# Window attention with group norm: x in eight transfers a block, y and output in row order, strided oT, another order of the prologue's transfers

## The chip, the cores and the metric

One core of a Trainium2 chip. The metric is the device time of one execution in microseconds (us); lower is better. The engines are PE (TensorE; PEld its weight loads), DVE (VectorE), ACT (ScalarE), POOL (GpSimd) and SP, which here only issues DMAs. ACT issues DMAs too; ACTq and SPq are their issue queues.

## The reference

```python
# x (8, 56, 88, 192) float32; windows of 7 x 11 tokens, 8 heads of 24
def _gn(v, G=32, eps=1e-05):      # over height, width and the 6 channels of a group
    ...
    return ((g - m) / jnp.sqrt(s + eps)).reshape(v.shape)
def _L0_conv_ref(x, qkv_w, qkv_b, proj_w, proj_b):
    ...
    qkv = xw @ qkv_w + qkv_b
    ...
    attn = jnp.einsum('bhnd,bhmd->bhnm', q, k) / jnp.sqrt(jnp.float32(hd)).astype(q.dtype)
    attn = jax.nn.softmax(attn, axis=-1)
    out = jnp.einsum('bhnm,bhmd->bhnd', attn, v)
    ...
    out = out @ proj_w + proj_b
    ...
return x + _L0_conv_ref(_gn(x), L0_conv_qkv_w, L0_conv_qkv_b, L0_conv_proj_w, L0_conv_proj_b)
```

## The kernel before

The 56 rows of an image are cut in four blocks of 14 rows (two strips of windows). A block has 16 windows of 77 tokens, worked on as eight pairs: a pair of windows, one above the other, is a step `i`, and there are 32 blocks and 256 steps. A block lies in SBUF with 112 partitions: one for each of its 14 rows and 8 window columns, in each of which are 11 tokens (tiles) of 192 channels.

Five engine programs run over the same `i`, each step of each engine working on another stage of the pipeline: x of step i+12 is normalised (POOL, L356, L358), that of i+11 split in two float16 parts (ACT L447, POOL L366, L367), that of i+10 transposed (PE L826) and copied out by ACT (L439). Steps 0, 1 and 2 of a block hold two tiles of x, the others one, as do the projections. For i come the scores (PE L758), their maximum (DVE L632), the transposed scores (L744) and their exponential `probs` (ACT L469); for i-1 probs times v (PE L731, `ps_a`), copied to `num` by ACT (L433). The sums of the exponentials go by DMA through DRAM and come back as inverses spread over 32 partitions each (`den`, `inv`, `inv_all`, SP). For i-8 POOL multiplies (`o`, L345), ACT writes the result's upper float16 part to `oT_hi` (L463) and POOL the lower part to `oT_lo` (L371). The output projection of a block (PE L698 into `ps_b`) starts when the oT of all its eight steps is there; DVE adds x, which is loaded a second time as `y_blk` (L640), and the store goes out from `y_blk`.

Float32 products are made of float16 parts in three to five passes; the weights are scaled and split in the prologue. Group statistics of image 0 are made in the prologue (`x_stat`, DVE L495), those of the others between the steps.

Transfers: ACT issues the x loads (L383) and the output stores (L387) after its `probs`, one of each in every second step; SP issues y (L283), statistics (L290) and the small ones. A block goes in four pieces of 4, 3, 2 and 2 tiles. In memory a row of the image is contiguous, and `x_blk`, `out_blk` and y's source take a block as window column, row, tile and channel, so that partition 14 w + r holds row r of window column w; `x_rows` has it as 8 r + w, in the order of memory. DMA and engine programs are kept in order by semaphores alone; the order of the instructions is that of the code.

```python
STEP_TILES = [(0, 2), (2, 2), (4, 2), (6, 1), (7, 1), (8, 1), (9, 1), (10, 1)]
PIECES = [(0, 4), (4, 3), (7, 2), (9, 2)]
```

## Time and profile before

| | |
|---|---|
| time, median of 3 runs | 1518.98 us (1517.67 to 1539.47) |
| the profiled execution: time, span | 1531.71 us, 1529.9 us |
| busy share: PE, PEld, DVE, ACT, POOL | 89%, 79%, 68%, 67%, 64% |
| granted clock, mean over the span | 0.971 |
| DMA | 170.36 MB, 111 GB/s on the mean |

The profiled execution is 1.8 us longer than its span and 12.7 us longer than the median. The granted clock is TensorE's, as a share of full speed. Idle time of an instruction stands in brackets or after a bar, with "<-" and what ended it; "issue" means that the profile shows nothing that the engine waited for. A window's row has the busy times of PE, PEld, DVE, ACT and POOL in this order, each with its instructions (x). The DMA share is the mean busy share of the core's 16 DMA engines. The prologue (weights, statistics of image 0) takes the first 66 us, the last projections and stores the time from 1490 us on.

### The profile page before, as it was taken

To read this page: it belongs to the slowest core of one execution; us is meant where nothing else is said; L and a number is where in the kernel's file an instruction comes from. 1 tells how busy PE (TensorE), PEld (TensorE's weight loads), DVE (VectorE), ACT (ScalarE), POOL (GpSimd) and SP (SyncE) were. 2 spreads that over 40 slices of the span, in tenths; PEclk is the share of its full clock that TensorE was granted. 3 is DMA by queue.
4 is the path that set the end of the run, shared out by engine and by line. 5 is a ranking of instruction groups with operands and counts; after the bars stand their busy time and mean duration, and the time that the engine had idled before them with its cause. 6 is when DMAs were issued, how large, how long until landed. Compare 5 with 4: busy or idle time off the path is not lost.

```text
span 1529.9 us, 84594 instructions
## 1 busy us (share of the span) xinstructions
PE 1361.8 (89%) x36832; PEld 1210.0 (79%) x36832; DVE 1047.8 (68%) x2227; ACT 1025.4 (67%) x1912; POOL 977.4 (64%) x1532
## 2 busy tenths in 40 slices
PE   0489899999998999999999989998999989999995
PEld 0377788888887888888888878887888878888884
DVE  5677677677766766777667866777667766666662
ACT  1567677766776677776767766776667666767761
POOL 0546766677665766767667776777667576767433
PEclk9999999999999999999999999999999999999997
DMA  7233344444444444444444443544433333433333
GB/s 211 69 95 88 112 114 129 120 118 124 108 128 100 115 129 104 129 107 132 111 114 134 113 108 108 132 123 116 116 99 97 98 95 89 106 95 93 85 84 105
DMA packets 129892, 170.36 MB, mean 111 GB/s; under 512 B 46898, under 2 KB 101490, under 8 KB 128628
## 3 DMA queue, kind: packets, MB, share of 16 engines
q1 hardware_dynamic: 98292, 100.59, 26.8%
q10 hardware_dynamic: 31232, 64.35, 14.0%
q8 instruction: 293, 4.80, 1.3%
q14 instruction: 75, 0.61, 0.1%
HBM read 132.04 MB, written 31.54 MB: 107 GB/s over the span
## 4 chain that ended last, share of the span: by engine, by line
PE 77%; DVE 8%; issue 6%; ACT 3%; POOL 3%; DMA 2%; SPq 1%; ACTq 0%; POOLq 0%; DVEq 0%
PE ps_a L698 13%; PE ps_b L698 13%; PE ps_q L698 11%; PE ps_k L698 11%; PE ps_a L731 10%; PE ps_s L744 8%; PE ps_s L758 5%; PE ps_k L826 4%; PE ps_q L793 3%; DVE neg_max L632 2%; POOL st_root L336 2%; DVE stat L495 2%; ACT probs L469 1%; DMA bias_in<-in_qkv_b 1%; DVE st_dev L510 1%
## 5 line engine op out<-in xcount | busy, mean ns | idle before, releaser
L632 DVE TENSOR_REDUCE neg_max<-ps_s 77x16 bf16<-77x1232 f32 x256 | 369.6, 1444 | 221.9 <-PE ps_s L758 221.1
L371 POOL TENSOR_TENSOR oT_lo<-o,oT_hi 128x308 f16<-128x308 f32 x256 | 193.7, 756 | 321.1 <-ACT oT_hi L463 321.1
L469 ACT ACTIVATE probs<-ps_s,exp_shift,exp_scale 77x1232 f32<-77x1232 f32 x256 | 349.2, 1364 | 9.9 <-PE ps_s L744 9.1
L731 PE MATMUL ps_a<-probs,v_all 77*32 77x77 f32 x8192 | 200.6, 234 | 41.1 <-issue 39.8
L452 ACT ACTIVATE v_all<-ps_a 77x384 f32<-77x384 f32 x256 | 124.9, 488 | 166.5 <-PE ps_a L698 166.4
L698 PE MATMUL ps_a<-wv_hiA,xT 128*128 128x192 f16 x1024 | 218.7, 253 | 2.5 <-issue 1.8
L345 POOL TENSOR_TENSOR o<-num,inv_all 128x308 f32<-128x308 f32 x256 | 216.2, 845 | 4.7 <-DMA inv_all<-den_dram 4.7
L439 ACT ACTIVATE xT<-ps_k 128x448 f16<-128x448 f16 x347 | 209.5, 642 | 8.9 <-PE ps_k L826 8.9
L731 PEld LDWEIGHTS ps_a<-probs,v_all 77*32 77x32 f32 x8192 | 148.7, 110 | 68.8 <-issue 44.4
L698 PE MATMUL ps_b<-wp_hi,oT_hi 128*112 128x192 f16 x694 | 188.1, 271 | 13.0 <-POOL oT_lo L371 6.8
L433 ACT ACTIVATE num<-ps_a 128x308 f32<-128x308 f32 x256 | 109.3, 427 | 133.0 <-PE ps_a L731 118.6
L698 PE MATMUL ps_k<-xT,wqk_hiA 128*128 128x154 f16 x1024 | 193.5, 236 | 0.0
L698 PE MATMUL ps_q<-xT,wqk_hiA 128*128 128x154 f16 x1024 | 186.0, 235 | 0.4 <-issue 0.3
L645 DVE TENSOR_TENSOR q_lo<-ps_q,q_hi 128x308 f16<-128x308 f32 x256 | 123.1, 481 | 89.4 <-PE ps_q L793 86.4
L649 DVE TENSOR_TENSOR k_lo<-ps_k,k_hi 128x308 f16<-128x308 f32 x256 | 123.1, 481 | 87.6 <-ACT k_hi L458 86.7
L458 ACT ACTIVATE k_hi<-ps_k 128x308 f16<-128x308 f32 x256 | 110.1, 430 | 106.5 <-PE ps_k L698 106.5
L698 PE MATMUL ps_b<-wp_lo,oT_hi 128*112 128x192 f16 x694 | 177.3, 255 | 0.2 <-issue 0.2
L698 PE MATMUL ps_b<-wp_hi,oT_lo 128*112 128x192 f16 x694 | 177.5, 256 | 0.0
L358 POOL TENSOR_TENSOR x_norm<-x_norm,rstd_all 112x384 f32<-112x384 f32 (+1 forms) x248 | 162.7, 656 | 19.4
L367 POOL TENSOR_TENSOR x_split<-x_norm,x_split 112x384 f16<-112x384 f32 (+1 forms) x248 | 170.2, 686 | 0.0
L356 POOL TENSOR_TENSOR x_norm<-x_norm,mean_all 112x384 f32<-112x384 f32 (+1 forms) x248 | 163.2, 658 | 4.1 <-issue 4.1
L366 POOL COPY x_split<-x_split 112x128 f16<-112x128 f16 (+1 forms) x248 | 64.1, 258 | 155.2 <-ACT x_split L447 154.8
(148 smaller groups left out, 3854.9 us busy)
## 6 DMA issues: line engine op xcount, KB each, us to landing
inv_all<-den_dram SPq DMA_DIRECT2D x1024, 38.5 KB
x_stat<-in_x SPq DMA_DIRECT2D x24, 504.0 KB, 6.1
x_norm<-in_x ACTq DMA_DIRECT2D x32, 336.0 KB
x_norm<-in_x ACTq DMA_DIRECT2D x64, 168.0 KB
y_blk<-in_x SPq DMA_DIRECT2D x32, 336.0 KB
y_blk<-in_x SPq DMA_DIRECT2D x64, 168.0 KB
out<-y_blk ACTq DMA_DIRECT2D x32, 336.0 KB
out<-y_blk ACTq DMA_DIRECT2D x64, 168.0 KB
```

The source lines that it names most:

```text
L345: nc.gpsimd.tensor_tensor(o32[o % 2][:, :], num[o % NUM_BUFS][:, :], inv_all[o % INV_BUFS][:, :], ALU.mult)\
L356: nc.gpsimd.tensor_tensor(x4, x4, of_group(mean_all, g, tiles), ALU.subtract).then_inc(pool_centred, 1)
L358: nc.gpsimd.tensor_tensor(x4, x4, of_group(rstd_all, g, tiles), ALU.mult).then_inc(pool_norm, 1)
L367: nc.gpsimd.tensor_tensor(xs[:, :, LO:ONE], x_step(x_norm, x_s), xs[:, :, 0:CH], ALU.subtract)\
L371: nc.gpsimd.tensor_tensor(oT_tokens(oT_lo, o), by_column(o32[o % 2]), oT_tokens(oT_hi, o), ALU.subtract).then_inc(pool_oT, 1)
L439: last = nc.scalar.activation(xT_tokens(parity(x_s), t0 + c), xT_psum(x_bank(x_s), c), ACT.Copy)
L452: nc.scalar.activation(v_all[v % V_BUFS][:, :, 0:HD], ps_a[0:TOK, 0:2 * CH].rearrange("p (h d) -> p h d", d=HD), ACT.Copy)\
L469: nc.scalar.activation(probs[i % 2][:, :, :].rearrange("p g (a n) -> p g a n", a=4), scores(), ACT.Exp, bias=exp_shift[0:TOK, :], scale=ex ...
L632: nc.vector.tensor_reduce(neg_max[:, :, :, HD:HD + 1].rearrange("p a g e -> p g (a e)"), scores(), AXIS.X, ALU.max, negate=True).then_inc( ...
L645: tt(heads(q_lo), heads(ps_q), heads(q_hi), ALU.subtract).then_inc(dve_q, 1)
L698: last = mm(dst, lhsT, rhs, start=first and n == 0, stop=n == len(pairs) - 1, skip_group_check=True)
L731: last = mm(o, v_all[s % V_BUFS][:, HEADS * w + NG * j + g, :], probs[s % 2][:, g, at:at + TOK], start=True, stop=True, skip_group_check=True)
```

## The change

The transfers of y and of the output take the block in the order of memory (partition 8 r + w). So that the projection's result comes out in that order, `oT_hi` and `oT_lo` are written with the window column innermost: a step's tokens lie 8 elements of float16 (16 bytes) apart, where they lay in runs of 14. x stays in the old order (partition 14 w + r), but is loaded in eight transfers of 14 partitions and 8448 bytes each, one for each window column, on one semaphore a block; two are issued in each of four consecutive steps, and the first of them waits until POOL has split the whole block before. In the prologue SP sends the qkv bias and the projection's weights ahead of its bias, ACT's second pair of statistics transfers waits for them, and the x of block 1 is issued after the weights are scaled. POOL's normalisation of block 1 waits for DVE's of block 0.

```diff
--- before.py
+++ after.py
@@ -93,7 +93,7 @@
 def window_attention(nc, x, qkv_w, qkv_b, proj_w, proj_b, out):
     x_rows = x.rearrange("b (s r) (w c) d -> (b s) (r w) (c d)", r=ROWS, c=WIN_W)
     x_blk = x.rearrange("b (s r) (w c) d -> (b s) w r (c d)", r=ROWS, c=WIN_W)
-    out_blk = out.rearrange("b (s r) (w c) d -> (b s) w r (c d)", r=ROWS, c=WIN_W)
+    out_rows = out.rearrange("b (s r) (w c) d -> (b s) (r w) (c d)", r=ROWS, c=WIN_W)
     den_dram = nc.dram_tensor("den_dram", (ROW_BUFS, NG, NUM), F32, kind="Internal").ap()
 
     with ExitStack() as ctx:
@@ -170,7 +170,7 @@
         dma_den = [sem(f"dma_den{p}") for p in range(DEN_BUFS)]
         dma_inv = [sem(f"dma_inv{p}") for p in range(DEN_BUFS)]
         dma_inv_all = [sem(f"dma_inv_all{p}") for p in range(INV_BUFS)]
-        dma_x = [[sem(f"dma_x{p}_{k}") for k in range(len(PIECES))] for p in range(2)]
+        dma_x = [sem(f"dma_x{p}") for p in range(2)]
         dma_y = [[sem(f"dma_y{p}_{k}") for k in range(len(PIECES))] for p in range(2)]
         dma_out = [[sem(f"dma_out{p}_{k}") for k in range(len(PIECES))] for p in range(2)]
         dma_stat = [sem(f"dma_stat{p}") for p in range(2)]
@@ -191,9 +191,9 @@
             t0, n = PIECES[k]
             return buf[:, t0:t0 + n, :].rearrange("p c d -> p (c d)")
 
-        def piece_of(rows, c, k):
+        def rows_of(rows, c, k):
             t0, n = PIECES[k]
-            return rows[c, :, :, t0 * CH:(t0 + n) * CH]
+            return rows[c, :, t0 * CH:(t0 + n) * CH]
 
         def stat_landed(g):
             return 16 * (2 * min(g + 1, 2) + 4 * max(g - 1, 0))
@@ -213,8 +213,7 @@
             return bank[:, at:at + 4 * PART].rearrange("p (k v r) -> p k v r", k=4, v=WINS)
 
         def oT_tokens(t, s):
-            at = (s % PAIRS) * 2 * WIN_H
-            return t[parity(s)][:, :, :, at:at + 2 * WIN_H].rearrange("p j c t -> p (j c) t")
+            return t[parity(s)][:, :, :, :].rearrange("p j c (t w) -> p (j c) t w", w=NWC)[:, :, :, s % PAIRS]
 
         def y_bank(r):
             return ps_q if r >= N_PAIRS - PAIRS and r % 2 else ps_b
@@ -238,14 +237,14 @@
             sp.dma_start(wA[:, :], qkv_w[0:CA, :]).then_inc(dma_w, 16)
             sp.dma_start(wB[0:CB, :], qkv_w[CA:CH, :]).then_inc(dma_w, 16)
             sp.dma_start(wB[CB:128, :], qkv_w[CA:CH, :]).then_inc(dma_w, 16)
-            sp.dma_start(bp[:, :], proj_b.rearrange("(a c) -> a c", a=1).broadcast_to([128, CH])).then_inc(dma_w, 16)
             sp.wait_ge(pool_const, 2)
+            b_row = qkv_b.rearrange("(a c) -> a c", a=1)
+            for row in (CB, CB + ROW_G):
+                sp.dma_start(bias_in[row:row + 1, :], b_row).then_inc(dma_rows, 16)
             p_rows = proj_w.rearrange("(j g d) c -> g d j c", g=NG, d=HD)
             for g in range(NG):
                 sp.dma_start(p32[ROW_G * g:ROW_G * g + HD, :, :], p_rows[g, :, :, :]).then_inc(dma_rows, 16)
-            b_row = qkv_b.rearrange("(a c) -> a c", a=1)
-            for row in (CB, CB + ROW_G):
-                sp.dma_start(bias_in[row:row + 1, :], b_row).then_inc(dma_rows, 16)
+            sp.dma_start(bp[:, :], proj_b.rearrange("(a c) -> a c", a=1).broadcast_to([128, CH])).then_inc(dma_w, 16)
             for h in range(2):
                 sp.wait_ge(stat_read, h + 1)
                 for n in range(2):
@@ -280,7 +279,7 @@
                 if r % 2 == 0 and 0 <= c < BLOCKS:
                     k = r // 2
                     reach(sp, dma_out[c % 2][k], 16 * (c // 2))
-                    sp.dma_start(piece(y_blk[c % 2], k), piece_of(x_blk, c, k)).then_inc(dma_y[c % 2][k], 16)
+                    sp.dma_start(piece(y_blk[c % 2], k), rows_of(x_rows, c, k)).then_inc(dma_y[c % 2][k], 16)
                 for h in range(2):
                     g, r = divmod(i + 67 - 16 * h, PAIRS_IMG)
                     if r % 3 == 0 and r <= 9 and 2 <= g < BATCH:
@@ -347,10 +346,12 @@
                 n = i + NORM_LEAD
                 if exists(n) and n >= PAIRS:
                     g = n // PAIRS_IMG
-                    if n % PAIRS_IMG == 0 or n == PAIRS:
+                    if n == PAIRS:
+                        pool.wait_ge(dve_norm0, 3)
+                    if n % PAIRS_IMG == 0:
                         pool.wait_ge(stats_done, g + 1)
-                    if n % 2 == 0:
-                        pool.wait_ge(dma_x[parity(n)][n % PAIRS // 2], 16 * (n // PAIRS // 2 + 1))
+                    if n % PAIRS == 0:
+                        pool.wait_ge(dma_x[parity(n)], NWC * 16 * (n // PAIRS // 2 + 1))
                     tiles = STEP_TILES[n % PAIRS][1]
                     x4 = x_step(x_norm, n).rearrange("p c (g k) -> p c g k", k=GCH)
                     nc.gpsimd.tensor_tensor(x4, x4, of_group(mean_all, g, tiles), ALU.subtract).then_inc(pool_centred, 1)
@@ -376,23 +377,28 @@
 
         @block.scalar
         def _(act):
-            def load_x(c, k):
+            def load_x(c, w):
                 if c == 2:
-                    act.wait_ge(dve_x0, 2 * k + 2)
-                reach(act, pool_x, PAIRS * (c - 3) + 2 * k + 2)
-                nc.scalar.dma_start(piece(x_norm[c % 2], k), piece_of(x_blk, c, k)).then_inc(dma_x[c % 2][k], 16)
+                    act.wait_ge(dve_x0, PAIRS)
+                reach(act, pool_x, PAIRS * (c - 2))
+                nc.scalar.dma_start(x_norm[c % 2][ROWS * w:ROWS * (w + 1), :, :].rearrange("p c d -> p (c d)"), x_blk[c, w, :, :])\
+                    .then_inc(dma_x[c % 2], 16)
+
+            def load_block(c):
+                for w in range(NWC):
+                    load_x(c, w)
 
             def store_y(c, k):
                 act.wait_ge(dve_out, PAIRS * c + 2 * k + 2)
-                nc.scalar.dma_start(piece_of(out_blk, c, k), piece(y_blk[c % 2], k)).then_inc(dma_out[c % 2][k], 16)
+                nc.scalar.dma_start(rows_of(out_rows, c, k), piece(y_blk[c % 2], k)).then_inc(dma_out[c % 2][k], 16)
 
             for h in range(2):
+                if h == 1:
+                    act.wait_ge(dma_rows, 6 * 16)
                 for n in range(2):
                     nc.scalar.dma_start(x_stat[h][:, n * TILES:(n + 1) * TILES, :].rearrange("p c d -> p (c d)"),
                                         x_rows[2 * h + n, :, :]).then_inc(dma_stat[h], 16)
-            for c in range(2):
-                for k in range(len(PIECES)):
-                    load_x(c, k)
+            load_block(0)
 
             def spread(t, rows=slice(0, 128)):
                 return t[rows, :, :, :].rearrange("p a g e -> p (a g) e")[:, :, 0:HD]
@@ -416,6 +422,7 @@
             nc.scalar.activation(wv["Bb"][top, :], wB[top, v], ACT.Copy)
             nc.scalar.activation(spread(wqk["Bb"], low), by_head(bias_in, low), ACT.Copy)
             nc.scalar.activation(wv["Bb"][low, :], bias_in[low, v], ACT.Copy).then_inc(act_w, 1)
+            load_block(1)
             act.wait_ge(stat_var, 1)
             nc.scalar.activation(st_log[:, :], st_var[:, :], ACT.Ln).then_inc(act_log, 1)
             act.wait_ge(act_log, 1)
@@ -469,9 +476,10 @@
                     nc.scalar.activation(probs[i % 2][:, :, :].rearrange("p g (a n) -> p g a n", a=4), scores(),
                                          ACT.Exp, bias=exp_shift[0:TOK, :], scale=exp_scale[0:TOK, :])\
                         .then_inc(act_exp, 1)
-                c, r = divmod(i + 18, PAIRS)
-                if r % 2 == 0 and 2 <= c < BLOCKS:
-                    load_x(c, r // 2)
+                c, r = divmod(i + 19, PAIRS)
+                if r < 4 and 2 <= c < BLOCKS:
+                    load_x(c, 2 * r)
+                    load_x(c, 2 * r + 1)
                 c, r = divmod(i - P_LAG - 2, PAIRS)
                 if r % 2 == 0 and 0 <= c < BLOCKS:
                     store_y(c, r // 2)
@@ -607,14 +615,11 @@
                 copy(xs[:, :, HI2:LO], xs[:, :, CA:CH])
                 tt(xs[:, :, LO:ONE], x_step(x_norm, step), xs[:, :, 0:CH], ALU.subtract).then_inc(dve_x0, 1)
 
-            dve.wait_ge(dma_x[0][0], 16)
+            dve.wait_ge(dma_x[0], NWC * 16)
             normalise(1, 0, 4)
-            dve.wait_ge(dma_x[0][1], 16)
             normalise(2, 4, 3)
             split_rest(0)
             split_rest(1)
-            dve.wait_ge(dma_x[0][2], 16)
-            dve.wait_ge(dma_x[0][3], 16)
             normalise(3, 7, 4)
             for step in range(2, PAIRS):
                 split_rest(step)
```

ACT in a middle block, from one pair of DMA issues on, before: `x_norm` is the loaded x, `in_x` the input.

```order
L383 DMA x_norm<-in_x 112x1x576
L387 DMA out<-y_blk 8x14x384
L433 ACTIVATE num<-ps_a 128x308
L439 ACTIVATE xT<-ps_k 128x4x16x7 x2
L447 ACTIVATE x_split<-x_norm 112x192
L452 ACTIVATE v_all<-ps_a 77x16x24
L458 ACTIVATE k_hi<-ps_k 128x4x77
L463 ACTIVATE oT_hi<-o_1 128x22x14
L469 ACTIVATE probs<-ps_s,exp_shift,exp_scale 77x1232
L433 ACTIVATE num<-ps_a 128x308
```

And after, at the second of the four steps that load:

```order
L384 DMA x_norm<-in_x 14x2112 x2
L393 DMA out<-y_blk 112x384
L440 ACTIVATE num<-ps_a 128x308
L446 ACTIVATE xT<-ps_k 128x4x16x7 x2
L454 ACTIVATE x_split<-x_norm 112x2x192
L459 ACTIVATE v_all<-ps_a 77x16x24
L465 ACTIVATE k_hi<-ps_k 128x4x77
L470 ACTIVATE oT_hi<-o_1 128x308
L476 ACTIVATE probs<-ps_s,exp_shift,exp_scale 77x1232
L384 DMA x_norm<-in_x 14x2112 x2
L440 ACTIVATE num<-ps_a 128x308
```

Each pair of one x load and one store has become two x loads with or without a store, or a store alone; the store's DRAM side of 8 by 14 rows is one of 112, and oT_hi's runs of 14 are one row of 308 elements with a step.

ACT in the prologue, before:

```order
L391 DMA x_stat<-in_x 112x2112 x4
L383 DMA x_norm<-in_x 112x1x768
L383 DMA x_norm<-in_x 112x1x576
L383 DMA x_norm<-in_x 112x1x384 x2
L383 DMA x_norm<-in_x 112x1x768
L383 DMA x_norm<-in_x 112x1x576
L383 DMA x_norm<-in_x 112x1x384 x2
L408 ACT_TABLE_LOAD
L408 ACTIVATE wA<-wA,big_inv 128x192 [waits dve_scales]
```

After, with the waits:

```order
L399 DMA x_stat<-in_x 112x2112 x2
L399 DMA x_stat<-in_x 112x2112 [waits dma_rows]
L399 DMA x_stat<-in_x 112x2112
L384 DMA x_norm<-in_x 14x2112 x8
L414 ACT_TABLE_LOAD
L414 ACTIVATE wA<-wA,big_inv 128x192 [waits dve_scales]
```

Block 1's loads have left this place; they stand behind the last of the weights' ACTIVATEs now, and a wait for the bias and projection weights stands ahead of the second half of the statistics.

## Rows read from the trace of the kernel before

**Rows 1.** The page of the kernel before, parts 1 and 3.

```profile
PE 1361.8 (89%) x36832; PEld 1210.0 (79%) x36832; DVE 1047.8 (68%) x2227; ACT 1025.4 (67%) x1912; POOL 977.4 (64%) x1532
...
q8 instruction: 293, 4.80, 1.3%
```

**Rows 2.** Who PE waited for, 60 to 1485 us: total us, times, longest us.

```profile
PE ps_a L731 <- issue: 39.8, 27, 3.7
...
PE ps_s L744 <- issue: 6.0, 7, 1.6
...
PE ps_k L826 <- issue: 5.2, 5, 2.3
```

**Rows 3.** Windows: us, busy of five engines, clock, DMA share, GB/s; PE's waits.

```profile
1100.00:1400.00 300.00, 283.30 (x7639) 254.34 (x7643) 197.82 (x369) 208.54 (x391) 197.97 (x317) 0.96 0.37 95
1400.00:1485.00 85.00, 83.54 (x2394) 74.78 (x2383) 58.92 (x102) 58.52 (x107) 41.14 (x64) 1.00 0.36 88
...
PE ps_s L758 <- ACT probs L469: 1.4, 7, 0.2
```

**Rows 4.** Timeline of ACT's issues and PE near 630 us; all of L383.

```profile
622.94 0.70 ACTq L383 DMA_DIRECT2D x_norm<-in_x  x1
...
623.68 0.69 ACTq L387 DMA_DIRECT2D out<-y_blk  x1
...
628.63 0.33 PE L731 MATMUL ps_a<-probs,v_all 77*32 77x77 f32 x7
630.72 0.66 PE L731 MATMUL ps_a<-probs,v_all 77*32 77x77 f32 x25 [1.75 <-issue]
...
L383 ACTq DMA_DIRECT2D x_norm<-in_x x128: 683/697/5037, 2.7 to 1398.9; - x128
```

**Rows 5.** Windows: two of the prologue, one at the lower clock.

```profile
742.20:745.40 3.20, 3.20 (x22) 3.11 (x21) 1.80 (x2) 1.15 (x3) 0.74 (x2) 0.50 0.33 83
10.00:17.00 7.00, 0.00 (x0) 0.00 (x0) 0.00 (x0) 0.00 (x0) 0.00 (x0) 1.00 1.03 288
18.50:28.00 9.50, 0.00 (x0) 0.00 (x0) 6.15 (x28) 1.28 (x1) 0.39 (x1) 1.00 0.53 194
```

**Rows 6.** The timeline of ACT and PE at the end of a step.

```profile
1459.25 0.45 ACT L463 ACTIVATE oT_hi<-o 128x308 f16<-128x308 f32 x1
...
1459.60 1.36 ACT L469 ACTIVATE probs<-ps_s,exp_shift,exp_scale 77x1232 f32<-77x1232 f32 x1
...
1461.11 0.32 PE L758 MATMUL ps_s<-k_hi,q_hi 25*128 25x77 f16 x16 [0.20 <-ACT probs L469]
```

**Rows 7.** DMA issues (KB each, us to landing); timeline of the prologue.

```profile
x_stat<-in_x ACTq DMA_DIRECT2D x4, 924.0 KB, 15.6
...
2.71 17.04 ACTq L383 DMA_DIRECT2D x_norm<-in_x  x8
...
21.71 0.35 DVE L559 TENSOR_REDUCE big_parts<-wA 128x1 f32<-128x192 f32 x1 [15.74 <-DMA bias_in<-in_qkv_b]
...
48.01 1.50 DVE L602 TENSOR_TENSOR x_norm<-x_norm,rstd_all 112x768 f32<-112x768 f32 x1
...
55.66 0.96 DVE L602 TENSOR_TENSOR x_norm<-x_norm,rstd_all 112x768 f32<-112x768 f32 x1
```

**Rows 8.** Groups by line and form, and two DVE memsets of the timeline.

```profile
L463 ACT ACTIVATE oT_hi<-o 128x308 f16<-128x308 f32 x256 | 117.6, 459 | 27.9 <-POOL o L345 27.9
L447 ACT ACTIVATE x_split<-x_norm 112x384 f16<-112x384 f32 x96 | 49.6, 518 | 2.4 <-DVE x_norm L602 2.4
...
L439 ACT ACTIVATE xT<-ps_k 128x448 f16<-128x448 f16 x347 | 209.5, 642 | 8.9 <-PE ps_k L826 8.9
...
L371 POOL TENSOR_TENSOR oT_lo<-o,oT_hi 128x308 f16<-128x308 f32 x256 | 193.7, 756 | 321.1 <-ACT oT_hi L463 321.1
...
1.24 0.07 DVE L546 MEMSET v_all<- 77x16 f32 x1
...
5.54 0.07 DVE L553 MEMSET big_parts<- 128x12 f32 x1
```

## The prediction

> **What bounds the kernel now.** I read the groups of PE's instructions first, then who made PE wait, then the ACT stretch between two steps, then the prologue. The work is 256 steps (one pair of windows each) of some 5.5 us between 66 us and 1490 us; PE is busy nearly all of it. In the late stretch from 1400 to 1485 us it is busy 83.54 of 85 us at a granted clock of 1.00; from 1100 to 1400 us only 283.3 of 300 us at 0.96 [rows 3]. So the steady part has two losses: idle time, and time at the lower of the two clock levels.
>
> The idle time has a pattern. Most of PE's waits end with no releaser ("issue"): 39.8, 6.0 and 5.2 us at the three places that hold most, 51.0 us in 39 waits, the longest 3.7 us [rows 2]. No data is missing there. One such wait stands in the middle of a run of 32 equal matmuls: 7 are issued, then nothing for 1.75 us, then the other 25 [rows 4]. What PE lacks is instructions. Queue q8 carried 293 packets with 4.80 MB, 16 KB each [rows 1]: with 36832 matmuls and as many weight loads on PE, that is one packet for every 251 of PE's instructions, so it brings PE's program, one every 5 us. It runs on the same DMA engines as the data. In the example ACT has issued an x load and an output store back to back at 622.94 and 623.68 us [rows 4], some 5 us before the wait. After the last x load, at 1398.9 us [rows 4], there is no wait of this kind up to 1485 us: the one row that the view of waits gives for that stretch is on ACT [rows 3], although stores and y loads go on and the DMA share is unchanged (0.36 against 0.37). So I read these waits as fetches that stand behind a pair of large ACT transfers.
>
> Why those transfers are slow shows in the prologue. From 10 to 17 us only whole-row transfers run (112 partitions on both sides) and the DMA share is 1.03 at 288 GB/s; from 18.5 to 28 us only x pieces run, and the share is 0.53 at 194 GB/s [rows 5]. An x piece uses half of the 16 engines; its DRAM side is written as 8 windows by 14 rows. y pieces and stores have the same shape. On each of these eight engines the queue is twice as long as it need be.
>
> The second thing that bounds a step is ACT's stretch k_hi, oT_hi, probs: they run back to back (oT_hi at 1459.25, probs at 1459.60 us), probs ends at 1460.96 and PE's next scores start at 1461.11 with an idle time of 0.20 us put down to probs [rows 6]. Anything added to oT_hi comes out at the end of the step, in the steps where PE gets there first. PE's L826 transposes are twice as many in three of eight steps, and there PE arrives later.
>
> **The change, part by part.**
>
> *Transfers.* y and output now have 112 rows on both sides, as the transfers of the 1.03 share had, so I take them to run on 16 engines with half the backlog on each. A block's x goes in eight transfers of 14 rows of 8448 bytes instead of four of 112 rows of 1536 to 3072 bytes: two in each of four consecutive steps. Two of them are 28 rows, two on each of 14 engines if the rows are spread evenly, where a piece put 14 rows on each of eight. Bytes per engine and step: before 14 x 3072 = 43 KB at most for each of x and store; after 17 KB and 21 KB. So the longest backlog falls from 86 to 38 KB, and the x load beside a store comes in two steps of eight instead of four. I take two thirds of the 51.0 us away: -34 us. Bounds: 0 (if fetches wait for something else) and -51.
>
> *The clock.* From 742.2 to 745.4 us, with PE busy throughout, the granted clock is 0.50, the level of 1.2 GHz [rows 5]. The mean of 0.96 against 1.00 [rows 3] is 12 us of full-speed work lost in 300 us, some 50 us over the 1300 us like it. Part follows waits on POOL's root of the statistics, which stay, and part is hidden where ACT is last. I take a sixth back, -8 us; bounds 0 and -25.
>
> *ACT's and SP's issue time.* An x piece takes ACT's queue 0.70 us, a store 0.69 [rows 4]. Now there are up to two x issues and a store in a step. Each whole row x issue is smaller; with the price unchanged it is 2.1 us beside a probs of 1.36 us and the wait before num, so at most some 0.5 us late in two of eight steps, 30 us in all if nothing hid it; with half the price nothing. I take 0: PE runs scores and projection before it needs num's bank. The added wait (all of block c-2 split before any of c is loaded) is met one step earlier by POOL; behind it on ACT would stand num and xT. The landing has seven steps, over 30 us, so one wait for eight transfers costs nothing.
>
> *Strided attention output.* ACT writes oT_hi and POOL reads it and writes oT_lo with 16 bytes from element to element instead of runs of 14. The trace has no such ACT or POOL instruction. Nearest rows [rows 8]: a DVE memset of 16 elements that lie 128 bytes apart takes 0.07 us, the same as one of 12 adjacent elements: a strided write at no cost. On ACT, 384 elements into long runs take 518 ns and 308 take 459, 0.78 ns each; by that xT's 448 in 64 runs of 7 should take 568 and take 642, 74 ns or 1.2 ns per run more. Charged to each of 308 single elements it is +0.36 us. So oT_hi costs 0 to +0.36 us; I take 0, by the DVE row, which is the only one with single elements. POOL waits 321.1 us for oT_hi in all, 1.25 us a step [rows 8]; that covers up to so much on its 756 ns. Where POOL is late (27.9 us of ACT's waits for it [rows 8]) a longer L371 adds to it: I take +3 us, bounds 0 and +10.
>
> *Prologue.* DVE's first reduction of the weights starts at 21.71 us, after an idle time ended by the DMA of bias_in [rows 7]. All four statistics transfers of 924 KB and all x pieces were queued beside the weights; ACT's eight x issues alone took 17.04 us [rows 7]. Now two statistics transfers (1.85 MB) and the weights with projection and biases (0.8 MB) come first, 2.65 MB at 288 GB/s [rows 5] = 9.2 us, from 2 us on, with 1.5 us for the last to land: 13 us instead of 21.7, -8.7 us. The second half of the statistics, then 6.4 us of transfer from 12 us on, is there by 20 us and wanted at 23; x block 0 by 25, wanted at 38. ACT issues block 1 after its weight work, where it waits for the variance anyway. POOL now waits for DVE's third normalisation: its first two block 1 steps start some 10 us later in the program, in an idle time of the same length. In exchange DVE's multiply of 768 elements is no longer beside POOL's: 1.50 us against 0.96 [rows 7]; with three more such steps I take -1.5 us. If the cover failed, POOL's two steps (5 us) would be the price. Sum -10, bounds -14 and -4.
>
> *Sum:* -34 - 8 + 0 + 3 - 10 = -49 us against the profiled execution of 1531.7 us. The median of the three timed runs is 12.7 us below it; such waits differ from run to run, and I take -45 against the median of 1519: **1474 us**.
>
> **What the Trainium skill says against it.** [Rows 2 to 4] show 51 us of fetch waits. "Runtime: NRT & Kernel Launch", Instruction fetch mechanics, says of crossing a 16 KiB boundary that it is "mostly hidden"; by that the term of -34 would be 0 and the result 1508 us. The 293 packets of 16 KB agree with its page size, the wait inside a run of matmuls speaks against "mostly hidden" here. "SBUF — State Buffer", on 16-byte cachelines, says that at least two accesses must fall in a line for full bandwidth, and that crossing to a new one at each access costs; oT's new step is exactly 16 bytes. The DVE row speaks against it for writes, with only 16 elements. Its outcome is the rival B.
>
> **The rivals.**
>
> *B, the strided write holds up ACT (ends slower at its upper price).* If each element of oT_hi takes two beats instead of one, the 0.78 ns per element of [rows 8] doubles: +0.24 us. ACT's stretch ends the step in about three quarters of the steps: 256 x 0.75 x 0.24 = +46 us: 1520 us. At the +0.36 us of xT's runs it is +69: 1543; with all steps charged, 1566. It makes the kernel slower than before from +0.23 us on. For it: the back-to-back stretch [rows 6]. Against: the DVE row.
>
> *C, no relief for fetches.* The backlog is not what delays them, or rows of 8448 bytes hold an engine as long as 14 small ones. Only the prologue and the POOL term remain: 1519 - 10 + 3 = 1512 us. For it: in no row is a fetch seen to wait. Against: the quiet stretch after the last x load [rows 3, 4].
>
> *D, POOL becomes the bound.* If L371 grows from 0.76 to 2.0 us or more, it uses up the 1.25 us a step; from there each 0.1 us costs 26 us: at 2.1 us 1500, at 2.3 about 1550.
>
> *E, the change does not do what it says:* y and output still on half the engines because of their SBUF side. Then half of the relief goes: 1495 us.
>
> **Chances.** Forecast 0.50 (with E's near half in its upper end; own range 1455 to 1492), B 0.22, C 0.17, D 0.05, E 0.06. Two per cent is 30 us, about what a measurement of this kernel tells from none: faster means under 1489, slower over 1549. The forecast lies below 1489 nearly always, E and C above it: faster 0.50. B at its lower price, C, E and a little of D are within: 0.38. B with the higher price, or with C (1558), and D: slower 0.12. The range from 1452 to 1545 leaves out about 0.05 below and 0.13 above.
>
> **What would show it.** First DVE reduction at about 13 us and its first multiply of x_norm at 39 instead of 48.01 us: prologue right. PE's "issue" waits at a third of 51 us, and a mean clock near 0.98 from 1100 to 1400: fetch right; unchanged: C. oT_hi's mean of 459 ns: at 460 the forecast, at 700 B. L371 under 1.2 us: no D. x_norm issues under 0.7 us each. Wrong would make it above all an oT_hi over 650 ns, or fetch waits that merely move to other transfers.

## The result and the profile after

The changed kernel takes **1664.7 us** (median of four runs, 1661.7 to 1670.5) against 1518.3 us for the kernel before on the same chip: ratio 1.097, 95% interval 1.093 to 1.102. It is slower by 146 us, far outside the range of the prediction. (Some executions of a kernel run over 1.5 per cent longer than its fastest at a lower clock; the ratios here and below leave them out, the medians don't.)

The page of the changed kernel: its span, the row of busy times, and the chain that ended last.

```profile
span 1659.9 us, 84721 instructions
...
PE 1346.2 (81%) x36832; PEld 1201.2 (72%) x36832; DVE 1045.9 (63%) x2227; ACT 1228.4 (74%) x1912; POOL 1097.6 (66%) x1532
...
PE 38%; ACT 26%; POOL 15%; issue 11%; DVE 4%; ACTq 3%; DMA 2%; SPq 0%; POOLq 0%; DVEq 0%
```

PE, which was busy 89 per cent of the span, is at 81, and it holds only 38 per cent of the chain, where the page of the kernel before has 77. The groups by line show whose work grew; these answer to [rows 8].

```profile
L372 POOL TENSOR_TENSOR oT_lo<-o,oT_hi 128x308 f16<-128x308 f32 x256 | 406.1, 1586 | 462.2 <-ACT oT_hi L470 462.2
...
L470 ACT ACTIVATE oT_hi<-o 128x308 f16<-128x308 f32 x256 | 405.4, 1583 | 33.4 <-POOL o L344 33.4
L476 ACT ACTIVATE probs<-ps_s,exp_shift,exp_scale 77x1232 f32<-77x1232 f32 x256 | 391.0, 1527 | 2.2 <-PE ps_s L749 1.2
...
L344 POOL TENSOR_TENSOR o<-num,inv_all 128x308 f32<-128x308 f32 x256 | 226.1, 883 | 0.0
```

oT_hi went from 459 to 1583 ns, oT_lo from 756 to 1586, with the same 308 elements each. probs, on which nothing was edited, went from a mean of 1.36 us (1364 ns) to 1.53 (1527).

PE's waits from 60 to 1610 us (engine, tile and line, who ended them: us in total, times, longest); they answer to [rows 2].

```profile
PE ps_s L763 <- ACT probs L476: 214.3, 242, 3.8
PE ps_a L736 <- issue: 2.3, 2, 1.7
PE ps_s L749 <- issue: 2.1, 3, 1.4
```

The "issue" waits have nearly gone: 7.2 us over all lines. In their place PE waits for probs in 242 of 256 steps. Here is one step end, the timeline at 700 us (start, duration, engine, idle time before in brackets), to be laid beside [rows 6].

```profile
700.02 0.43 ACT L465 ACTIVATE k_hi<-ps_k 128x308 f16<-128x308 f32 x1 [0.34 <-PE ps_k L703]
700.35 1.58 ACT L470 ACTIVATE oT_hi<-o 128x308 f16<-128x308 f32 x1
701.41 1.55 ACT L476 ACTIVATE probs<-ps_s,exp_shift,exp_scale 77x1232 f32<-77x1232 f32 x1
...
703.10 0.32 PE L763 MATMUL ps_s<-k_hi,q_hi 25*128 25x77 f16 x16 [0.90 <-ACT probs L476]
```

Before, probs started 0.35 us behind the start of oT_hi; now it starts 1.06 us behind. It also lasts 0.16 us (by the means) to 0.19 us (here) longer. Together that is 0.9 us on the stretch that ends the step, and PE's idle time went from 0.20 to 0.90 us. (The record of probs begins before that of oT_hi has ended: by 0.10 us in [rows 6], by 0.52 us here. So not all of the 1.12 us by which oT_hi grew is seen.)

The windows that answer to [rows 3] (window, length, busy PE, PEld, DVE, ACT, POOL, granted clock, DMA share, GB/s):

```profile
1100.00:1400.00 300.00, 253.29 (x7004) 227.33 (x7002) 191.29 (x384) 230.03 (x357) 211.50 (x291) 0.98 0.37 94
1400.00:1485.00 85.00, 72.80 (x2052) 65.59 (x2044) 50.50 (x86) 67.93 (x108) 61.32 (x88) 1.00 0.38 95
```

Even with the clock at 1.00 and no "issue" waits, PE is busy 72.80 of 85 us, where it was 83.54.

The prologue, in the timeline, did what was forecast; it answers to [rows 7].

```profile
13.99 0.35 DVE L567 TENSOR_REDUCE big_parts<-wA 128x1 f32<-128x192 f32 x1 [8.01 <-DMA bp<-in_proj_b]
...
14.64 3.68 ACTq L384 DMA_DIRECT2D x_norm<-in_x  x8
...
40.30 0.96 DVE L610 TENSOR_TENSOR x_norm<-x_norm,rstd_all 112x768 f32<-112x768 f32 x1
```

And the DMA issues by line (durations in ns: least, median, most):

```profile
L384 ACTq DMA_DIRECT2D x_norm<-in_x x256: 320/396/1774, 14.6 to 1481.0; - x128
...
L393 ACTq DMA_DIRECT2D out<-y_blk x128: 322/340/2107, 170.8 to 1657.3; - x128
```

An x issue takes ACT's queue 0.40 us and a store 0.34, where they took 0.70 and 0.69 [rows 4].

### The profile page after: what moved, and what is told of

It reads as the page before. It is cut to its first block, busy times and chain, and to the rows that moved or that the text cites. A ratio compares the mean times of both kernels' runs of the same rounds, so it can differ in the third digit from the quotient of the medians.

```text
span 1659.9 us, 84721 instructions
## 1 busy us (share of the span) xinstructions
PE 1346.2 (81%) x36832; PEld 1201.2 (72%) x36832; DVE 1045.9 (63%) x2227; ACT 1228.4 (74%) x1912; POOL 1097.6 (66%) x1532
## 4 chain that ended last, share of the span: by engine, by line
PE 38%; ACT 26%; POOL 15%; issue 11%; DVE 4%; ACTq 3%; DMA 2%; SPq 0%; POOLq 0%; DVEq 0%
ACT probs L476 15%; PE ps_b L703 11%; ACT oT_hi L470 10%; PE ps_a L703 10%; PE ps_k L703 9%; POOL oT_lo L372 7%; PE ps_s L763 4%; POOL st_root L335 2%; PE ps_q L798 2%; DVE neg_max L637 2%; POOL x_norm L359 2%; POOL x_split L368 2%; POOL x_norm L357 2%; ACTq L384 1%; POOL o L344 1%
## 5 line engine op out<-in xcount | busy, mean ns | idle before, releaser
L372 POOL TENSOR_TENSOR oT_lo<-o,oT_hi 128x308 f16<-128x308 f32 x256 | 406.1, 1586 | 462.2 <-ACT oT_hi L470 462.2
L470 ACT ACTIVATE oT_hi<-o 128x308 f16<-128x308 f32 x256 | 405.4, 1583 | 33.4 <-POOL o L344 33.4
L476 ACT ACTIVATE probs<-ps_s,exp_shift,exp_scale 77x1232 f32<-77x1232 f32 x256 | 391.0, 1527 | 2.2 <-PE ps_s L749 1.2
L763 PE MATMUL ps_s<-k_hi,q_hi 25*128 25x77 f16 x4096 | 84.9, 197 | 219.3 <-ACT probs L476 215.4
L763 PEld LDWEIGHTS ps_s<-k_hi,q_hi 25*128 25x128 f16 x4096 | 56.8, 94 | 259.6 <-issue 252.4
L344 POOL TENSOR_TENSOR o<-num,inv_all 128x308 f32<-128x308 f32 x256 | 226.1, 883 | 0.0
L703 PE MATMUL ps_a<-wv_hiA,xT 128*128 128x192 f16 x1024 | 214.2, 249 | 0.6 <-issue 0.2
L736 PE MATMUL ps_a<-probs,v_all 77*32 77x77 f32 x8192 | 193.9, 234 | 2.4 <-issue 2.3
```

The costliest lines, as they stand in the source:

```text
L344: nc.gpsimd.tensor_tensor(o32[o % 2][:, :], num[o % NUM_BUFS][:, :], inv_all[o % INV_BUFS][:, :], ALU.mult)\
L372: nc.gpsimd.tensor_tensor(oT_tokens(oT_lo, o), by_column(o32[o % 2]), oT_tokens(oT_hi, o), ALU.subtract).then_inc(pool_oT, 1)
L470: nc.scalar.activation(oT_tokens(oT_hi, o), by_column(o32[o % 2]), ACT.Copy).then_inc(act_oT, 1)
L476: nc.scalar.activation(probs[i % 2][:, :, :].rearrange("p g (a n) -> p g a n", a=4), scores(), ACT.Exp, bias=exp_shift[0:TOK, :], scale=ex ...
L703: last = mm(dst, lhsT, rhs, start=first and n == 0, stop=n == len(pairs) - 1, skip_group_check=True)
L736: last = mm(o, v_all[s % V_BUFS][:, HEADS * w + NG * j + g, :], probs[s % 2][:, g, at:at + TOK], start=True, stop=True, skip_group_check=True)
```

## The experiments

Twelve kernels ran. "Theory 1" below is throughout: ACT's f16 write at 16 bytes a step is dear by itself, and costs the step because it stands on ACT's back-to-back stretch.

**The forms by themselves.** No kernel around them: on each engine four instructions in a row of 128 x 308 elements from an f32 tile, for each distance between written elements, with one engine at work at a time. The rest of the computation is left out.

```diff
+ for s in (1, 2, 4, 7, 8, 16):
+     for _ in range(REPEATS):
+         link(act, nc.scalar.activation(every(f16["act"][s], s), src[:, :], ACT.Copy))
+ for s in (1, 2, 4, 8):   # ... the same into f32, then a strided f16 read; DVE and POOL likewise
```

> A kernel that only copies x to the output and, with nothing beside it, runs single operations on 128 x 308 elements one after the other: ACT copies, DVE casts and POOL subtractions that write float16 at a step of 1, 2, 4, 7, 8 and 16 elements and float32 at 1, 2, 4 and 8, and such that read float16 at 1, 4 and 8. It computes nothing of the attention. Theory 1 (a strided write is dear by itself): ACT at step 8 takes about 1.58 us, as oT_hi does in the changed kernel, against 0.46 at step 1; POOL's write at step 8 takes about 1.5 us and its read at most 1.1. Theory 2 (the price comes from ACT and POOL working on lines of the same tile at the same time): ACT at step 8 stays under 0.8 us here. Theory 3 (16-byte lines decide): float16 is cheap up to step 4 and dear from 8, float32 dear from step 4. Theory 4 (any gap decides, single 2-byte writes): float16 is dear from step 2 on and float32 never.

Windows of four instructions each on ACT (window, length, busy time of the four, clock, DMA): f16 written at a step of 1, 2, 4, 8 and 16 elements, and f32 at 8.

```profile
124.40:126.46 2.06, 1.84 (x4) 1.00 0.00 0
126.46:128.79 2.33, 2.19 (x4) 1.00 0.00 0
128.79:132.45 3.66, 3.54 (x4) 1.00 0.00 0
...
138.13:144.51 6.38, 6.25 (x4) 1.00 0.00 0
144.51:150.60 6.09, 5.96 (x4) 1.00 0.00 0
157.68:160.82 3.14, 3.01 (x4) 1.00 0.00 0
```

Divided by four: 460, 547, 885, 1562 and 1490 ns in f16, 753 in f32. The 1562 ns at step 8 (16 bytes) are within 2 per cent of the 1583 of the kernel, without any other engine at work, so theory 2 fell. The same on POOL: f16 at step 1, f16 at step 8, f32 at step 8.

```profile
167.50:171.34 3.84, 3.07 (x4) 1.00 0.00 0
184.41:190.94 6.53, 6.22 (x4) 1.00 0.00 0
207.35:210.76 3.41, 3.10 (x4) 1.00 0.00 0
```

768, 1555 and 775 ns. On DVE a cast of the same shape takes 321 ns at step 1 and 848 at step 8 in f16 (windows of four: 1.28 and 3.39 us), and 443 in f32 at step 8. So the price lies in the write itself, and most of it in the f16 type; neither contention nor the addressing of single elements alone explains it, since POOL writes f32 at 32 bytes for 7 ns more. Theories 3 and 4 both fell too: in f16 ACT's time rises at every distance instead of at one (547 ns at 4 bytes, 885 at 8), and f32 is dearer on ACT (753 ns) and DVE (443) but not on POOL. Why the types differ is open.

**oT in runs, all else as changed.** oT_hi and oT_lo are written in runs of 14 as before while y and output stay in row order, so tokens meet the wrong rows: the output is not the reference's.

```diff
-            return t[parity(s)][:, :, :, :].rearrange("p j c (t w) -> p (j c) t w", w=NWC)[:, :, :, s % PAIRS]
+            at = (s % PAIRS) * 2 * WIN_H
+            return t[parity(s)][:, :, :, at:at + 2 * WIN_H].rearrange("p j c t -> p (j c) t")
```

> The changed kernel with oT_hi and oT_lo written in runs of 14 elements as before, everything else as changed. The projection's rows then meet the y of other tokens, so the output is not the reference's; the amount of work is the same. Theory 1: all of the loss is the strided write and what my prediction gave for the rest holds: 1474 us, between 1455 and 1492, PE's waits without releaser under 20 us. Rival (the new transfers or waits cost too): above 1519 us.

Measured 1495.7 us, ratio to before 0.982 (0.978 to 0.985). The strided oT costs some 170 us (169 between the medians on two chips, 176 by the two ratios), more than the 146 by which the kernel got slower: the rest of the change is worth 1.8 per cent. That is less than expected: the time lies above the range up to 1492, and the "issue" waits above 20 us. PE's "issue" waits from 60 to 1485 us fell from 62.0 us (all lines, the largest in [rows 2]) to 40.5. Its largest rows:

```profile
PE ps_s L750 <- issue: 17.2, 14, 4.4
PE ps_s L764 <- ACT probs L477: 15.3, 16, 2.1
PE ps_a L737 <- issue: 8.5, 7, 2.8
```

**x and prologue as changed, y, output and oT as before.**

```diff
-                nc.scalar.dma_start(rows_of(out_rows, c, k), piece(y_blk[c % 2], k))
+                nc.scalar.dma_start(piece_of(out_blk, c, k), piece(y_blk[c % 2], k))
```

(and the same for y's loads, with oT in runs)

> The changed kernel with y, output and oT as before (8 by 14 rows, runs of 14); only x in eight transfers and the new prologue are left of the change. Prologue alone would give 1519 - 10 = 1509 us. If fetches of instructions wait behind pairs of x load and store, half of those pairs are gone and x is on 14 engines: about 1485 us and some 25 us of PE waits without releaser. If only y and stores mattered: 1509 us and 50 us of such waits.

1524.5 us, ratio 1.002 (0.997 to 1.008), above both 1485 and 1509. First probs came at 65.7 us instead of 75.1, and still nothing was gained; "issue" waits were 62.0 us, as before. So x in eight transfers relieves no fetch, and costs about what the prologue gives.

**Row order and strided oT on the kernel before** (x in four pieces, old prologue).

```diff
-            return t[parity(s)][:, :, :, at:at + 2 * WIN_H].rearrange("p j c t -> p (j c) t")
+            return t[parity(s)][:, :, :, :].rearrange("p j c (t w) -> p (j c) t w", w=NWC)[:, :, :, s % PAIRS]
```

> The kernel before with y and output in row order and the strided oT, x still in four pieces and the old prologue. Theory 1: the strided write is the loss, so it comes out above the changed kernel by the prologue's 10 us: about 1675 us, PE's wait for probs above 200 us. Rival (x in eight transfers or its wait on a whole block carries part of the loss): under 1650 us.

1675.8 us, as theory 1 had it, ratio 1.100 (1.096 to 1.104), with oT_hi at 1584 ns, oT_lo at 1585 and PE waiting 207 us for probs. This part alone makes the whole loss.

**The prologue alone** on the kernel before.

```diff
+            for k in range(len(PIECES)):      # behind ACT's weight work; block 0 stays in front
+                load_x(1, k)
             act.wait_ge(stat_var, 1)
```

(and SP's order, the wait ahead of the second half of the statistics and POOL's wait, as in the change)

> The kernel before with the new prologue alone (SP's order of the weights' transfers, the second half of the statistics behind the projection and biases, x block 1 behind ACT's weight work, POOL's first block 1 step behind DVE's third normalisation); x in four pieces, y and output by window. If the prologue's gain is real and only the eight transfers of x cost time in the run x8_and_prologue (ratio 1.0023 with both), this is 9 to 11 us faster than before: 1508, ratio 0.993, first probs at 65 to 66 us instead of 75.1, and the eight steps of a block add up to 41.0 us as before. If the gain is given back later by something in the steady part whatever x does, it is level: 1518.

1518.3 against 1534.7 us on that chip, ratio 0.989 (0.986 to 0.993): the prologue's gain, 16 us by the ratio (11 to 22), is there and is kept; it is somewhat more than the 9 to 11 expected. First probs at 65.3 us.

**One strided write at a time.** First ACT's alone, with POOL writing oT_lo in runs, so that the lower parts stand at other tokens than the upper ones; then POOL's alone, with ACT writing in runs, so that the upper parts stand at the wrong tokens.

```diff
-                    nc.gpsimd.tensor_tensor(oT_tokens(oT_lo, o), by_column(o32[o % 2]), oT_tokens(oT_hi, o),
+                    nc.gpsimd.tensor_tensor(oT_runs(oT_lo, o), by_column(o32[o % 2]), oT_tokens(oT_hi, o),
```

> The changed kernel, but POOL writes oT_lo in runs of 14 (it still reads oT_hi strided); ACT writes oT_hi strided. The output is not the reference's. Theory 1 (ACT's strided write alone holds the step, since it stands on ACT's back-to-back stretch): oT_hi stays at about 1.58 us, oT_lo falls to 1.0 us, and the time stays within 25 us of the changed kernel, 1640 to 1665. Rival (POOL's own strided write is what the steps wait for, or is needed too): at least half of the 146 us goes, 1590 or less. PE's waits for probs: about 200 us by the first, under 100 by the second.

> The changed kernel, but ACT writes oT_hi in runs of 14 and POOL reads it so; POOL alone writes oT_lo strided. The output is not the reference's. Theory 1 (ACT's write is what costs): oT_hi 460 ns, oT_lo 1.5 to 1.6 us, and the time within 20 us of rows_in_runs' 1496, since POOL had 1.25 us a step to spare. Rival (each strided write alone costs, by a shared path of the two engines or by POOL's pace): 1560 or more, with probs still at 1.5 us.

ACT's alone: 1649.8 us. POOL's alone: 1503.0. The groups of ACT's alone, and its largest wait:

```profile
L474 ACT ACTIVATE oT_hi<-o 128x308 f16<-128x308 f32 x256 | 405.2, 1583 | 30.4 <-POOL o L348 30.4
L480 ACT ACTIVATE probs<-ps_s,exp_shift,exp_scale 77x1232 f32<-77x1232 f32 x256 | 390.7, 1526 | 2.5 <-PE ps_s L753 1.7
L376 POOL TENSOR_TENSOR oT_lo<-o,oT_hi 128x308 f16<-128x308 f32 x256 | 254.2, 993 | 513.8 <-ACT oT_hi L474 513.8
...
PE ps_s L767 <- ACT probs L480: 212.6, 241, 3.5
```

and the groups of POOL's alone:

```profile
L376 POOL TENSOR_TENSOR oT_lo<-o,oT_hi 128x308 f16<-128x308 f32 x256 | 408.2, 1594 | 235.5 <-ACT oT_hi L474 235.3
...
L474 ACT ACTIVATE oT_hi<-o 128x308 f16<-128x308 f32 x256 | 117.6, 459 | 30.7 <-POOL o L348 30.7
```

The first is 15 us below the changed kernel, the second 7 us above the kernel with neither. These are single runs on two chips; set against before on their own chips (medians 1534.7 and 1519.1 us) they are 1.075 and 0.989, beside 0.982 with neither, which gives some 142 us for ACT's write and 12 for POOL's. POOL's instruction grew by 838 ns, but from its start to that of `o` behind it, it is only 1.19 us instead of 0.72, since their records overlap by 0.4 us: some 120 us in all. That found room in idle time: POOL's waits for oT_hi fell from 312.3 us (oT in runs) to 235.3, those for x_split from 134.0 to 93.0. On ACT the start of the next instruction moves by 0.72 us, and there it costs 142 to 154 us. probs is at 1.53 us in the first and not in the second, so it goes with ACT's own strided write ahead of it, not with POOL's beside it. Whether probs works longer, or its record only holds more of the overlap with oT_hi, no run tells apart; PE waits for its end in either case.

**The reordering moved to f32.** The microbenchmark says where the order can be changed for nothing: in POOL's f32 product. o32 becomes a buffer of a whole block in row order, and oT_hi and oT_lo are made tile by tile one step before the projection, both from and to adjacent elements.

```diff
-                    nc.gpsimd.tensor_tensor(o32[o % 2][:, :], num[o % NUM_BUFS][:, :], inv_all[o % INV_BUFS][:, :], ALU.mult)
+                    nc.gpsimd.tensor_tensor(o32_step(o), by_column(num[o % NUM_BUFS]), by_column(inv_all[o % INV_BUFS]), ALU.mult)
...
-                    nc.scalar.activation(oT_tokens(oT_hi, o), by_column(o32[o % 2]), ACT.Copy).then_inc(act_oT, 1)
+                    nc.scalar.activation(oT_tiles(oT_hi, t), o32_tiles(t), ACT.Copy).then_inc(act_oT, 1)
```

Here t = i - 15; o32_step is the strided view of one step, o32_tiles the adjacent view of the one or two tiles that step t of the projection takes.

> The changed kernel with the reordering moved to the f32 product: POOL writes o32 in row order at 32 bytes a step into a buffer of a whole block (in the microbenchmark 775 ns strided against 768), and one step before the projection wants them, ACT and POOL make oT_hi and oT_lo of one or two tiles from and to adjacent elements. Theory 1 (only the f16 writes at 16 bytes were dear): oT_hi's mean is 450 to 480 ns, the first product's stays within 5 per cent of 883 ns, and the time is that of rows_in_runs, 1495 (ratio 0.98). Rival: the strided f32 write is dearer beside the other engines than alone, or PE now waits each step for oT_lo of the step before, 0.2 us a step or more: 1545 or slower, with PE's waits for POOL oT_lo at 50 us.

1498.4 us, ratio 0.978 (0.974 to 0.982), and nothing is left out: the time of the kernel with oT in runs, as theory 1 had it. oT_hi's mean is 451 ns. The rival fell by its own marks (1545 us, 50 us of waits), but it saw something: PE does wait 31.7 us for oT_lo, though most of it in seven waits of 3 us and not in each step.

**The same with x in four pieces and the new prologue.**

```diff
-                    pool.wait_ge(dma_x[parity(n)], NWC * 16 * (n // PAIRS // 2 + 1))
+                    pool.wait_ge(dma_x[parity(n)][n % PAIRS // 2], 16 * (n // PAIRS // 2 + 1))
```

> As g1_staged_rows, but x comes in four pieces as before, with the new prologue. If x in eight transfers costs 0.4 to 0.6 us a block in the steady part (13 to 18 us), this is that much faster than g1_staged_rows: 1478 to 1484, ratio 0.975, and a block's eight steps add up to 40.9 us or less instead of 41.4. If x's eight transfers are what relieves the fetches when y and output take 16 engines, PE's issue waits are back at 60 us and it is at 1495 or above. If the row order of y and output gives the relief, they are 40 us or less.

1489.1 us, ratio 0.970 (0.966 to 0.973): 9 us less than with eight transfers on the same chip, somewhat less than the 13 to 18 expected, and the "issue" waits are 34 us. The row order of y and output gives the relief; x in eight transfers takes some of it back.

**One step of slack.** In that kernel's timeline POOL is late once an image:

```profile
680.21 5.43 POOL L348 TENSOR_TENSOR st_root<-st_var,half_power 112x32 f32<-112x32 f32 x1
...
688.16 1.03 POOL L386 TENSOR_TENSOR oT_lo<-o,oT_hi 128x448 f16<-128x448 f32 x1
...
689.34 0.26 PE L716 MATMUL ps_b<-wp_hi,oT_hi 128*112 128x192 f16 x1 [3.03 <-POOL oT_lo L386]
```

```diff
-P_LAG = PAIRS + O_LAG
-T_LAG = P_LAG - 1
+T_LAG = PAIRS + O_LAG - 1
+P_LAG = T_LAG + 2
```

The store hangs on P_LAG and the x load does not. So this edit also moves the stores into the steps without an x load: in the timeline of the kernel without slack they are issued at 704.14 (x) and 704.88 us (store), with slack at 704.51 and 709.76. It is two changes in one, which the expectation does not hold.

> g2_staged_rows_x4 with one step more between oT_lo and the projection (projection, y and output one step later, so one more step at the end). In its trace PE waits for oT_lo 20 us in seven waits, six of them some 3.0 us, one per image, each behind POOL's root of 5.4 us. If that wait was a price of the tight handover, it goes: -18 us, +2 to 3 us for the step at the end, ratio 0.957 to 0.962. Rival: POOL is then late for something else just as long (num's inverse product, x_split) or PE's neighbour waits take its place: ratio 0.970 as before.

**x loads in the steps without a store**, on the kernel without slack.

```diff
-                c, r = divmod(i + 18, PAIRS)
+                c, r = divmod(i + 17, PAIRS)
```

> g2_staged_rows_x4 with x's pieces issued one step later, in the steps that have no store (before, load and store stood in the same step). If a fetch waits because an x load and a store are queued together, PE's issue waits fall from 35 us to 20 or less and the ratio from 0.970 to 0.960. Rival: what counts is that an x piece on half the engines is under way at all: the waits stay at 30 to 40 us and the ratio at 0.970.

Both ran on one chip, on which the kernel before scattered from 1483 to 1531 us, so the two are best set against each other, the more so as x loads and stores are apart in both and only the slack differs (projection, y and store a step later): 1433.8 us with slack (1425.5 to 1438.8), 1466.8 with x in odd steps (1465.4 to 1475.5). The ratios are 0.961 (0.955 to 0.967) and 0.985 (0.979 to 0.990). Against the median of all eleven executions of before on that chip (1519.1) they are 0.944 and 0.966. The 0.961 is what was forecast for the slack, but the move of the stores is in it too; 1433.8 us is the shortest time of this study, and that kernel leaves nothing out. The waits for oT_lo, from 60 us to the end of the steps, are gone with slack; with x in odd steps they are as they were:

```profile
PE ps_b L716 <- POOL oT_lo L386: 20.6, 7, 3.0
```

The cores' view (span, mean granted clock) of the kernel with slack, and of the one with x in odd steps:

```profile
core 0: 1433.0 us, clock 0.988
```

```profile
core 0: 1463.8 us, clock 0.979
```

Of the 31 us between these spans, 20.6 are the waits for oT_lo, and (1 - 0.979) x 1463.8 - (1 - 0.988) x 1433.0 = 14 us are the clock; "issue" waits (21 against 24 us) and the added step go the other way. The trace shows where those 14 us come from. Here are, with x in odd steps, the 2 us ahead of the end of one wait (3.04 us, to 511.13), the 8 us behind it, and the 8 us behind the only one of the seven that lowered nothing:

```profile
509.10:511.10 2.00, 0.00 (x0) 0.00 (x1) 1.14 (x1) 0.36 (x1) 2.00 (x5) 0.74 0.76 209
511.13:519.13 8.00, 8.00 (x147) 7.34 (x148) 3.23 (x9) 2.78 (x5) 4.21 (x8) 0.64 0.14 40
682.72:690.72 8.00, 8.00 (x220) 7.31 (x224) 5.49 (x12) 4.42 (x9) 5.50 (x11) 1.00 0.30 78
```

PE does 147 matmuls where it does 220 at 1.00. The clock of the 8 us behind the seven waits is 0.64, 0.80, 0.64, 1.00, 0.69, 0.82 and 0.83, 12.6 us lost in all. So removing seven waits brought two thirds of their length again in clock, which my -18 did not hold. It is not one execution's luck: the six with slack ran at 0.985 to 0.994, the six with x in odd steps at 0.975 to 0.981.

With x in odd steps the "issue" waits are 21 us instead of 34. That is on the side of "load and store queued together delay a fetch", though it missed my bound of 20 by one. With slack, where load and store are apart too, they are 24 us, which is on the same side. The ratio (0.985, forecast 0.960) says the contrary, the spans (1463.8 against 1486.3 us, on two chips) say a gain as forecast. The waits' sign is what I keep; the gain in time stays open.

**x in eight transfers alone** on the kernel before.

```diff
-                nc.scalar.dma_start(piece(x_norm[c % 2], k), piece_of(x_blk, c, k)).then_inc(dma_x[c % 2][k], 16)
+                nc.scalar.dma_start(x_norm[c % 2][ROWS * w:ROWS * (w + 1), :, :].rearrange("p c d -> p (c d)"), x_blk[c, w, :, :])\
+                    .then_inc(dma_x[c % 2], 16)
```

> The kernel before with x in eight transfers of one window each alone; old prologue, y and output by window. If x in eight transfers costs 0.5 us a block (the run with the prologue was level, the prologue alone 1.1 per cent faster), this is 10 to 20 us slower than before: ratio 1.007 to 1.013. Rival (the two runs stood on different chips and the cost is smaller than that difference; between the two staged kernels it was 0.8 per cent): ratio 1.000 to 1.006.

1552.4 us (1529.8 to 1561.0), ratio 1.029 (1.017 to 1.041); against all runs of before on that chip (median 1519.1) it is 1.022. It is slower than either theory had it. Some 8 us are the old prologue with sixteen issues instead of eight (first probs at 82.8 us, against 75.1). The rest is in the steps, where PE's "issue" waits are 61 us, as before, and the mean clock is 0.964 against 0.971. From the first probs to the last it is 1430.9 us against 1419.4; of these 11.5 us the difference of the clocks (0.007) would be 10, but the two profiles were not taken together. The cause is not settled: all three pairs (this one, 1.002 against 0.989 with the new prologue, 0.978 against 0.970 with staged oT) have the sign; their sizes are 33 us between the medians (8 of them the prologue), 20 us and 9 us.

## Why the prediction was wrong

**The failed step is the price of oT_hi**: "oT_hi costs 0 to +0.36 us; I take 0, by the DVE row". It measured +1.12 us, of which 0.72 reach the start of probs, and probs grew by 0.16. The bound itself failed, not only the choice in it. The DVE row was of 16 elements of f32 written 128 bytes apart by a memset: too few to show a price per element, another type, another engine. At DVE's own price of a strided f32 element, (443 - 321) / 308 = 0.4 ns, it would have shown 6 ns in 70. In f32 a stride of 32 bytes costs 7 ns on POOL and 293 ns on ACT; in f16 one of 16 bytes costs 787 and 1102 ns. The upper end, xT's runs of seven, had six of seven elements next to the one before. Neither row held what was decisive, narrow elements each written alone, and I should have left the upper end open instead of calling +0.36 a bound.

**Rival B had the mechanism**, but not the size: it priced the write at +0.24 to +0.36 us and ended at 1520 to 1566. "ACT's stretch ends the step in about three quarters of the steps": 242 of 256 show the wait. What reaches the end of the step is +0.72 us by which probs starts later and +0.16 by which it lasts longer. PE's waits for probs went from 15.3 us (oT in runs) to 214.3, by 199 us; of that 33 us only take the place of "issue" waits (40.5 with oT in runs, 7.2 now), and some 8 that of time at the lower clock ((1 - 0.971) x 1496.5 against (1 - 0.979) x 1659.9). This gives 158 us; between these two profiled spans lie 163.4.

**The Trainium skill's rule on 16-byte lines** ("SBUF — State Buffer", Door 1: The DMA port swizzle, the note on cachelines) was cited against the change and then outweighed by the DVE row. For f16 the runs bear it out that an access to a new line each time is dear, on all three engines; on ACT it is 460, 547, 885 and 1562 ns at 2, 4, 8 and 16 bytes, and no more at 32 (1490). Its threshold, that two accesses in a line suffice, does not hold here (885 ns at 8 bytes, two in a line), and POOL's f32 at 32 bytes, at 775 ns, does not follow it at all.

**Rival D (POOL the bound) fell**: L372 at 1.59 us stayed under the 2.0 us from which I had it decide, and alone it cost 7 to 12 us; I had +3 for the term.

**Fetch waits, -34.** Two thirds of 51 us in the three rows was too much: with oT in runs all "issue" waits went from 62.0 to 40.5 us, a third. The relief came from y and output alone; x's part of the step, the "17 KB" on 14 engines, gave none (62.0 us still). The grouping holds in every profile without ACT's strided write: 59.5 to 62.0 us with y and output by window (before, x and prologue, prologue alone, x alone), 21 to 44 us with them in row order. That these waits are for instructions, which I had inferred from q8's packets, the trace's DMA records show: in the kernel before all 38 "issue" waits of 0.5 us or more from 80 to 1485 us (56.6 of the 62.0 us) end 1.2 to 1.7 us behind the end of a q8 packet, where such packets come every 4.6 us (median) and only 5 of 36 waits put down to another engine end so. These packets took 1.0 us, like the others of q8; they came late and were not slow themselves. What holds them back is argued from the grouping and from the two kernels with load and store apart, not seen. In the changed kernel only 7.2 us are seen, presumably because a PE that waits for ACT in each step hides them (10.5 us with ACT's write alone strided, 43.9 with POOL's). That is also why the row that I had named as the mark of a right prediction, these waits at a third of 51, came true in a kernel that lost.

**Clock, -8.** With oT in runs the profiled execution, the slowest of four, had a mean clock of 0.971, like before; the four together ran at 0.971 to 0.979 (median 0.977) and the seven of before on that chip at 0.969 to 0.978 (0.972). That is some 7 us, about the term, though the ranges overlap. In the changed kernel it is 0.98 from 1100 to 1400 us, as I had put it, in a kernel that lost.

**Prologue, -10**: right in the trace, and somewhat short in time. The first reduction stands at 13.99 us (13 forecast), the multiply at 40.30 (39) and at 0.96 us, the first probs came 10.2 us earlier; alone it gave 16 us by the ratio, with an interval from 11 to 22.

**ACT's and SP's issue time, 0**: each issue fell to about half, as supposed. Yet x in eight transfers cost 9 us or more, a loss that no term had. **Rival E** fell: y and output in row order did relieve the queues. **Rival C** was half right: no relief from x.

The sum with what the runs gave: prologue -16, "issue" waits -21, clock -7 and x in eight transfers some +20 are -24 where oT in runs measured 27 below before (1495.7 against 1523.2 on that chip), instead of my -45; and some 170 us of strided write that I had at 3.

## What to carry to other kernels

Price a changed access pattern with the instruction's own type, element count and engine, four in a row in a small kernel, before arguing from a row of another shape; a "nearest row" with 16 elements bounds nothing. When an order has to change somewhere, change it where the write measures cheap (here POOL's in f32) and the engine has slack: the same row order of y and output cost 10 per cent when ACT wrote it in f16, and with POOL writing it in f32, a block ahead, the kernel was 3 to 4 per cent faster than before, the prologue's one per cent among them. And ask of each handover what the producer's longest job is: POOL's root of 5.4 us, once an image, reached PE as 3 us each time until there was a step of slack. And when a lag changes, look at what else hangs on it: the slack also moved the stores away from the x loads.

## What the hardware showed that I had not expected

- An f16 write at 16 bytes a step takes 3.4 times as long as an adjacent one on ACT (1562 against 460 ns for 308 elements), 2.0 times on POOL (1555 against 768), 2.6 times on DVE (848 against 321). In f32 at 32 bytes it is 1.6, 1.01 and 1.4 times.
- ACT reading f16 at 16 bytes a step takes 742 ns against 460, so on ACT the write is dearer than the read. Behind its strided write the next instruction's record is longer too: probs 1364 to 1527 ns, with POOL's writes strided or not.
- A wait of PE can cost more than its length: behind six of seven waits of 2.5 to 3.0 us the granted clock was at 0.50 for a while (0.64 to 0.83 over the next 8 us, PE busy throughout), and without them the time lost at the lower clock was 14 us less, on the same chip.
- PE's "issue" waits are waits for its program: all 38 of 0.5 us or more in the kernel before end 1.2 to 1.7 us behind the end of a packet of the instruction queue q8.
